# Attention with split operands: four key tiles in parts instead of two, and one rotated projection per chunk

## The reference, cut to what matters

```
x: (4, 1024, 256), 16 heads of 128
xn  = layernorm(x)
qkv = xn @ w_qkv.T;  q, k rotated (rope)
attn = softmax(q k^T / sqrt(128)) v            per sequence and head
ffn  = gelu(xn @ mxfp4(up) + up_bias) @ mxfp4(down) + down_bias
out = x + attn @ w_out.T + ffn
```

## Time and profile before

| | |
|---|---|
| median of 3 runs | 2452.34 us (2449.78 to 2453.95) |
| the profiled execution, its own time | 2450.13 us |
| its span in the profile | 2448.3 us |
| PE busy | 99% of the span |
| DVE, POOL, ACT busy | 78%, 71%, 69% |
| granted TensorE clock | 0.998 of full speed |

### The profile page before, as it was taken

One profiled execution on the slowest core, in us unless ns is written; L12 is line 12 of the kernel. 1 busy time (PEld: TensorE's weight loads), 2 busy tenths in 40 slices (PEclk: granted clock), 3 DMA queues, 4 the chain that ended last, 5 costly groups with the idle time before them and its releaser, 6 DMA issues. The chain is left out here.

```text
span 2448.3 us, 42812 instructions
## 1 busy us (share of the span) xinstructions
PE 2417.7 (99%) x13168; PEld 2124.8 (87%) x13168; DVE 1912.9 (78%) x2671; ACT 1677.9 (69%) x3039; POOL 1728.9 (71%) x1358
## 2 busy tenths in 40 slices
PE   6999999999999999999999999999999999999999
PEld 5888888888888888888888888888888888888888
DVE  6778788777877877787787778778777877877776
ACT  7767777776766777676677767667776766777533
POOL 4778877777777777777777777777777777777331
PEclk9999999999999999999999999999999999999999
DMA  4766666667666666667666666667676565666742
GB/s 140 185 170 161 171 158 178 162 162 195 182 161 149 158 152 157 157 148 195 179 161 153 157 157 148 161 149 183 165 186 157 148 162 149 157 153 161 230 153 69
DMA packets 400878, 396.72 MB, mean 162 GB/s; under 512 B 38656, under 2 KB 383104, under 8 KB 400768
## 3 DMA queue, kind: packets, MB, share of 16 engines
q1 hardware_dynamic: 400768, 395.67, 63.0%
HBM read 91.43 MB, written 35.65 MB: 52 GB/s over the span
## 5 line engine op out<-in xcount | busy, mean ns | idle before, releaser
L947 DVE TENSOR_REDUCE neg_max<-s_ps 128x1 f32<-128x1024 f32 x512 | 621.0, 1219 | 291.2 <-PE s_ps L1244 290.5
L1244 PE MATMUL s_ps<-seq_parts 128*128 128x512 f32 x3072 | 826.8, 408 | 1.4 <-DVE seq_parts L1111 0.8
L758 ACT ACTIVATE probs<-s_ps,neg_max 128x1024 f32<-128x1024 f32 x512 | 570.6, 1114 | 365.5 <-DVE neg_max L947 361.8
L1326 PE MATMUL o_ps<-keys_first,v_rows 128*128 128x256 f32 x3072 | 707.7, 380 | 1.3 <-ACT v_rows L725 1.3
L957 DVE STREAM_TRANSPOSE turned_blocks<-probs 128x1024 f32<-128x1024 f32 x512 | 630.6, 1237 | 60.6 <-ACT probs L758 38.1
L1244 PEld LDWEIGHTS s_ps<-seq_parts 128*128 128x128 f32 x3072 | 571.8, 188 | 117.2 <-ACT probs L758 1.5
L1326 PEld LDWEIGHTS o_ps<-keys_first,v_rows 128*128 128x128 f32 x3072 | 566.9, 190 | 68.6 <-ACT v_rows L725 1.7
L608 POOL TENSOR_TENSOR keys_first<-keys_first,seq_parts 128x512 fp32r<-128x512 f32 x256 | 332.4, 1298 | 320.2 <-ACT seq_parts L764 320.0
L587 POOL TENSOR_TENSOR rope_a<-rope_a,cos 128x512 f32<-128x512 f32 x252 | 325.3, 1291 | 176.9 <-ACT rope_b L740 176.7
L601 POOL TENSOR_TENSOR seq_parts<-rope_a,seq_parts 128x512 fp32r<-128x512 f32 x252 | 359.4, 1426 | 95.2 <-ACT seq_parts L750 95.1
L1244 PE MATMUL slot_ps<-seq_parts,w_parts 128*128 128x512 f32 x1506 | 387.9, 393 | 0.0
(11 more groups left out here) (118 smaller groups left out, 2597.2 us busy)
## 6 DMA issues: line engine op xcount, KB each, us to landing
keys_first<-turned_blocks SPq DMA_DIRECT2D x2048, 128.0 KB, 2.7
w_parts<-w_qkv_parts SPq DMA_DIRECT2D x72, 512.0 KB, 4.3
w_qkv_parts<-w_parts SPq DMA_DIRECT2D x24, 512.0 KB, 3.7
wo_parts<-w_out_parts SPq DMA_DIRECT2D x48, 256.0 KB, 3.1
seq_parts<-xnt_parts SPq DMA_DIRECT2D x16, 512.0 KB, 4.6
w_raw<-in_w_qkv SPq DMA_DIRECT2D x24, 256.0 KB, 4.1
seq_parts<-xnt_parts SPq DMA_DIRECT2D x6, 1024.0 KB, 8.5
y<-in_x SPq DMA_DIRECT2D x16, 256.0 KB, 3.2
```

Of the source, the lines that this page charges most:

```text
L758: nc.scalar.activation(probs[:, k2 % 4, :], s_ps[k2 % 2][:, :], ACT.Exp, bias=neg_max[:, col:col + 1], accum_out=row_sum[:, col:col + 1]). ...
L947: nc.vector.tensor_reduce(neg_max[:, k2 % 16:k2 % 16 + 1], s_ps[k2 % 2][:, :], AXX, ALU.max, negate=True).then_inc(max_ready, 1)
L1244: ins = nc.tensor.matmul(out, w, m, start=(n == 0), stop=(n == len(terms) - 1))
L1326: last = nc.tensor.matmul(out, v_rows[:, parity, kt - SPLIT, cols], keys_first[:, slot, :, kt, :].bitcast(F32), start=False, stop=(kt == B ...
```

## The change

`SPLIT` goes from 2 to 4. So `values` takes four key tiles in parts and four as f32; `probs_high` and `probs_low` each work on 1024 columns in one instruction; a second of the four v groups gets a low part on DVE; and `p_hi` and `v_lo` fill their memory, so that the feed-forward part can no longer begin before the last chunk: `G_SLOT` goes, the steps 16 and 17 keep one `up` each, and every `gelu` and `split_gelu` and all `down`s come after the steps.

`GROUPS` is written anew so that each step has one rotated group. ACT takes it, POOL makes `rotated_low` of the group before and `rotated_sum` of this one (`SUM_AT`, `LOW_AT`), and ACT makes `rotated_high` of it as the last thing of the step, now behind `probs_high`. The order of the first chunks stays (`FIRST_LATER`). Some weight and input loads move by one step.

```diff
-SPLIT = 2
+SPLIT = 4
...
-        GROUPS = {(2, 1): (0, "qk0", 0), (3, 1): (1, "qk0", 1), (4, 0): (2, "qk0", 2), (4, 1): (3, "v", 0),
-                  (5, 0): (4, "qk0", 3), (6, 0): (5, "v", 1), (6, 1): (6, "qk1", 0), (7, 0): (7, "v", 2),
-                  (7, 1): (8, "qk1", 1), (0, 0): (9, "qk1", 2), (0, 1): (10, "qk1", 3), (1, 0): (11, "v", 3)}
+        GROUPS = {(1, 1): (0, "qk0", 0), (2, 1): (1, "qk0", 1), (3, 1): (2, "qk0", 2), (4, 0): (3, "v", 0),
+                  (4, 1): (4, "qk0", 3), (5, 0): (5, "qk1", 0), (6, 0): (6, "v", 1), (6, 1): (7, "qk1", 1),
+                  (7, 0): (8, "v", 2), (7, 1): (9, "qk1", 2), (0, 0): (10, "v", 3), (0, 1): (11, "qk1", 3)}
+        SUM_AT = {2: ("qk0", 0), 3: ("qk0", 1), 4: ("qk0", 2), 5: ("qk0", 3), 6: ("qk1", 0), 7: ("qk1", 1), 0: ("qk1", 2), 1: ("qk1", 3)}
+        LOW_AT = {(k + 1) % 8: g for k, g in SUM_AT.items()}
...
POOL, a step (after probs_low):
-                if k8 == 0:
+                if first and k == 0:
                     rotated_low(p, "qk1", 0)
                     rotated_sum(p, "qk1", 1)
                     rotated_sum(p, "qk1", 2)
...
+                else:
+                    if k8 < 3 or more_pairs:
+                        rotated_low(p if k8 < 3 else p + 1, *LOW_AT[k8])
+                    if k8 < 2 or more_pairs:
+                        rotated_sum(p if k8 < 2 else p + 1, *SUM_AT[k8])
...
+                if k8 == 3 and more:
+                    w_low(p + 1, "qk1")
                 if k8 == 3 and splitting:
                     wo_low(p, 1)
-                if k8 == 4 and more:
-                    w_low(p + 1, "qk1")
...
ACT, a step (w_high of qk1 moves from step 4 to step 3; after the second exponential):
-                    if k % 8 == 3 and more_pairs:
-                        rotated_high(p + 1, "qk0", 0)
...
+                    if g and k % 8 == 5:
+                        take(0, g)
+                    probs_high(i, k)
+                    if first and k == 0:
                         rotated_high(p, "qk1", 1)
-                    if last and k == 15:
-                        act.wait_ge(bias_loaded, 32)
-                        act.wait_ge(blocks_turned, TOK * HEADS // P - 3)
-                        gelu(0, 0, True)
-                        gelu(0, 1, True)
-                        high_out(c - 1, 0)
-                    probs_high(i, k)
+                    elif k % 8 < 2 or more_pairs:
+                        rotated_high(p if k % 8 < 2 else p + 1, *SUM_AT[k % 8])
...
PE, the last steps:
-                if last and k == 15:
-                    up(0, 0, 0)
-                    up(0, 0, 1)
-                elif tail and k == 16:
-                    up(0, 0, 2)
-                    pe.wait_ge(mx_w_loaded[1], 32)
-                    pe.wait_ge(probs_ready, TOK * HEADS // P)
-                    down(0, 0, 0)
-                elif tail:
-                    down(0, 0, 1)
+                if tail:
+                    up(0, 0, k - 16)
...
-                if tail and k == 16:
-                    up(0, 0, 3)
...
+            pe.wait_ge(mx_w_loaded[1], 48)
+            pe.wait_ge(probs_ready, TOK * HEADS // P)
```

More of the change, by code:

```diff
@@ L244, in layer, with group_at @@
         V_SPLIT = tuple(n for n in range(4) if V_TILES[n] < SPLIT // 2)
-        USED = {"qk0": 5, "v": 12, "qk1": 11}
+        USED = {"qk0": 5, "v": 12, "qk1": 12}
         LN_SLOT, MX_SLOT = (5, 1), (13, 1)
         MX_PARTS = {0: (2,), 2: (3,), 3: (4,), 6: (5,), 7: (6, 7), 8: (8, 9), 10: (10,), 11: (11,), 12: (12,), 15: (0, 1)}
-        def group_at(k, slot, last):
+        def group_at(k, slot, last, first=False):
+            if first and (k, slot) in FIRST_LATER:
+                return (*FIRST_LATER[k, slot], 0)
             g = GROUPS.get((k % 8, slot))
@@ L255, in group_at @@
                 return None
-            ahead = k // 8 + (1 if k % 8 >= 2 else 0)
+            ahead = k // 8 + (1 if k % 8 >= 1 else 0)
             if last and ahead > 1:
@@ L654, in step @@
                     rotated_sum(p, "qk1", 2)
-                if k8 == 1:
+                elif first and k == 1:
                     rotated_low(p, "qk1", 1)
@@ L723, in take_group @@
                     at = 2 * V_TILES[n]
+                    tiles = bank.rearrange("p (a b) -> p a b", a=2)
                     rows = v_hi[:, parity, at:at + 2, :] if n in V_SPLIT else v_rows[:, parity, at - SPLIT:at - SPLIT + 2, :]
-                    nc.scalar.activation(rows, bank.rearrange("p (a b) -> p a b", a=2), ACT.Copy).then_inc(v_ready, 1)
+                    nc.scalar.activation(rows, tiles, ACT.Copy).then_inc(v_ready, 1)
                     return
@@ L854, in step @@
                     w_high(p + 1, "v")
+                if k % 8 == 3 and more:
+                    w_high(p + 1, "qk1")
                 if k % 8 == 3 and splitting:
                     wo_high(p, 1, first)
-                if k % 8 == 4 and more:
-                    w_high(p + 1, "qk1")
                 if k % 8 == 6 and more:
                     wo_high(p + 1, 0)
-                if tail:
-                    if k == 16:
-                        gelu(0, 2, True)
-                        gelu(0, 3, True)
-                    else:
-                        high_out(c - 2, k % 2)
-                    return
                 if not (first and k < 2):
@@ L875, in take @@
                     take_group(i * 2 + g[3], *g[:3], g[3] % 2, slot_ps[:, slot])
-                g_before = None if tail or (first and k == 0) else group_at(k - 1, 1, last)
-                if g_before and k % 8 != 1:
+                g_before = None if tail or (first and k == 0) else group_at(k - 1, 1, last, first)
+                if g_before and not (first and k == 1):
                     take(1, g_before)
@@ L933, in gelu @@
                                      bias=up_bias[:, f:f + 1]).then_inc(gelu_ready, 1)
-            steps_splitting(act, step)
-            for f in range(4, FT):
+            act.wait_ge(bias_loaded, 32)
+            act.wait_ge(blocks_turned, TOK * HEADS // P)
+            for f in range(FT):
                 gelu(0, f, True)
@@ L1195, in step @@
                         quantise(i + 1, part)
+            steps(dve, step)
             def split_gelu(g, f, first):
@@ L1224, in group @@
                 g, first = b * 2 + n, isinstance(b, int) and b == 0 and n == 0
-                for f in range(4 if first else 0, FT):
+                for f in range(FT):
                     split_gelu(g, f, first)
@@ L1268, in bank_free @@
             def bank_free(i, k, slot, first, last):
[L1271 removed]
+                for kk in (k - 1, k - 2, k - 3, k - 4):
                     if first and kk < 0:
@@ L1279, in bank_free @@
                         return
-                    g = group_at(kk % 16, slot, last and kk >= 0)
+                    g = group_at(kk % 16, slot, last and kk >= 0, first)
                     if g:
@@ L1452, in slot @@
                         return
-                    g = group_at(k, n, last)
+                    g = group_at(k, n, last, first)
                     if not g:
@@ L1495, in group @@
             def group(b, n, final):
-                for f in range(2 if b == 0 and n == 0 else 0, FT):
+                for f in range(FT):
                     if f < FT - 2:
```

68 lines of the change are left out of this document (14 added, 54 removed).

## The result

The change made the kernel slower: 2532.93 us median of four runs against 2451.65, a ratio of 1.0327 [1.0301, 1.0354]. The forecast was 2428 (2415 to 2446), so it has the wrong sign. The profiled execution took 2531.62 us, its span 2529.8.

What follows compares the result with a forecast made beforehand. PE's instruction stream was taken as the bound: -37.9 + 6 + 1.5 + 1.5 + 4.5 = -24.4 us against the profiled 2450.1 gives 2425.7; with 2.2 for the median of the runs, 2428 us, range 2415 to 2446.

Steps and rivals of the forecast that it cites:

- What bounds the kernel: Whole kernel: the length of PE's instruction stream sets the time, nearly alone; PE busy for 99% of the span.
- what PE gains: PE's values: two key tiles go from f32 to parts, 0.148 us less per chunk, 37.9 us in all.
- Parts at the f32 rate: Rival on PE's values: a part costs half an f32 instruction, 0.108 us, giving 2411 us; chance 0.03.
- no gain: Rival on PE's values: six more parts cost what four f32 instructions did, so PE saves nothing, 2464 us; chance 0.03.
- Durations off PE: ACT and POOL, per chunk: probs_high +0.49 us at 1024 columns, probs_low taken as 2.5 us.
- Is a one-group step kept?: One-group steps, sequences 1 to 3: POOL's 7.8 us fit in 8.03, high_out is on time, no loss.
- DVE held up by POOL: Rival: a third of some 80 two-input DVE instructions in one-group steps cost PE 0.5 us each, +13, 2441 us; chance 0.06.
- The hard ring: Rival, one-group steps: POOL's sum delays rotated_high, high_out and PE by 0.4 us each, giving 2478 us; chance 0.10.
- The first sequence: Steps 2 and 3 there: added weight low parts put POOL behind, PE waits 0.7 to 0.8 us a pair, +6 us.
- The start: First chunk: its low part comes 1.2 + 0.5 us later, but a wait for v stood behind; +1.5 us.
- The end: Last seven chunks without projection, +1.5 us as probs_high's extra length shows, and feed-forward work losing its cover, +4.5 us.
- the seam: Between last chunks and feed-forward part: two pieces come behind and PE waits for the first down; +4.5 us (3 to 8).

Runs made afterwards that it cites:

- places8: early8 with VectorE's quantisation comparisons spread, two instead of three in steps 7 and 8, one more each in steps 9 and 10: 2437.04 us, ratio 0.9941.
- six: Changed kernel with newton on POOL, low parts halved, quantisation in two-group steps, and six instead of eight transfers per chunk from the fifth: 2467.30 us.
- no_newton: Changed kernel without newton's four small VectorE operations, the normalisation taking the unrefined guess: 2493.51 us, ratio 1.0153.
- loop7: Changed kernel with newton on POOL, low parts halved, quantisation in two-group steps, and the loops' turn moved from step 4 to 7: 2485.62 us.
- early8: early with the loops' turn moved to step 8: 2468.42 us, ratio 1.0073.
- two mends of A: Against the changed kernel: newton moved to POOL, 2500.74 us; probs_low as two operations of 512 columns, 2496.14 us; both together, 2492.86 us.
- shadow: Changed kernel with rotated_high ahead of probs_high again and POOL's sum ahead of rotated_low: 2524.45 us, ratio 1.0303.
- six mends: On the changed kernel: newton on POOL, low parts halved, quantisation moved, probs_high per key tile, turn in step 8, comparisons spread: 2437.04 us.
- early: Changed kernel with newton on POOL, low parts halved, quantisation in two-group steps, and probs_high in two operations, one per key tile's transfers: 2481.97 us.

## Why the prediction was wrong

*What bounds the kernel, and what PE gains*: right. The stream shrank by 0.131 a step, 0.140 in a one-group step (8.033 for 8.173), against 0.148 forecast; over 256 chunks 34 instead of 37.9 us. Parts at the f32 rate and "no gain" are both out. Where nothing else is in the way (places8) the gain is there.

*Durations off PE*: right (`p_hi` +0.43 for +0.49, `probs_low` 2.41 for 2.5).

**The step that failed** is "Is a one-group step kept?", where it says that POOL starts early, "when `p_hi` comes", that `rotated_high` ends near 7.4 us, "before the step does; `high_out` behind it is then on time", and "in sequences 1 to 3 I count no loss". I took `p_hi` to come at any time that suits POOL. It can't start before its transfer lands: in the trace of before it ended a wait for the DMA 7.57 us into a step (at 1569.86), in the rows of after above 7.76 us into one. What the diff puts behind it comes later by that much: in steps 3 `high_out` starts at a median of 1.64 us, where before it was 0.39. This was to be read from the trace of before: ACT waited for that DMA 52 times, 56.6 us, with `rotated_high` in the shadow of the wait and `high_out` at 0.39. I counted the lengths of ACT's list and not the time from which it may run, and I didn't list SP's eight issues. The landing alone is worth about 22 us (six).

**The second** is the size of "DVE held up by POOL", given 0.06 and +13 us. The mechanism was right and the population wrong: I priced L1037's kin at 0.5 us each for a third of 80. The costliest are not these but newton's four operations on two columns, absent from my list because they took 0.12 to 0.17 where POOL was idle; behind a busier POOL they take 5.3 us a round, and alone are worth 39 us (no_newton). The Trainium skill, "GPSIMD Engine Reference", Key points, says that POOL shares its SBUF interfaces with VectorE and contends there with VectorE instructions that have two SBUF inputs or run in a 2-port mode; the traces agree with a contention, and show that a waiting operation ends within 0.03 us of POOL's instruction, whatever its own size. The forecast's word on `v_low`, "nothing, unless DVE is late there", is of the same kind: it asked what the new operation adds, not what the old ones meet.

**The third**, not in the prediction at all, is the turn of the loops: 20.0 us in ten gaps in ACT, much as before the change (21.9), but without slack behind it now, and 11.7 us in eight gaps in PE itself, where before there were none. Moving it alone was worth 4 us (loop7) or 14 (early8). What makes PE's gaps appear stays open.

*The hard ring*, my main rival, ended on the right side for a wrong reason: ACT's wait for POOL's sum went down, from 79.7 to 16.7 us, and POOL had 50 of 300 us free. *The first sequence*: +6 was forecast, and without the other causes 9.9 us more than before are late in all sequences together (places8), 7.8 of them in the first. *The start* was +5.2, not +1.5: PE waits 8.11 us for a projection's bank and goes on at half clock (its six matmuls take 2.93 us), where before it waited 3.13 and 1.25 us. *The end*: forecast +1.5 + 4.5, less 1.2 that the eight last chunks save, 4.8; measured 3.3 (places8 4.2). The rows of the start and of the seam, where a gelu is waited for 0.65 and a split 0.23 us:

```profile
57.39 2.93 PE L1210 MATMUL slot_ps<-seq_parts,w_parts 128*128 128x512 f32 x6 [8.11 <-ACT rope_b L734]
...
2405.87 1.15 PE L1330 MATMUL s_ps<-seq_parts,up_w 128*128 128x512 f32 x4 [0.65 <-ACT probs L905]
2407.25 1.22 PE L1343 MATMUL s_ps<-w_parts,seq_parts 128*128 128x256 f32 x8 [0.23 <-DVE seq_parts L1173]
```

One sum of the forecast was off by itself: "no gain" is 2450.1 + 13.5 + 2.2 = 2466 us, not 2464; nothing hangs on it.

How the causes share the 105 us of added late time isn't known, and may be no sum: two mends of A that gave 32 and 37 us alone gave 40 together, and newton's lock is worth 6 us in the kernel before and 39 in the changed one. Whether VectorE's small operations are free of the lock with their operands in PSUM wasn't tried, and neither was a transfer of fewer, larger pieces.

## What to carry to other kernels

For each operation that is moved, write down not only how long the engine's list is but what its first instruction waits for, transfers and their issue times above all: work ahead of such a wait is covered by it, the same work behind it makes what follows late by its length (though moving it back, in shadow, gained 8 us only, since the other engines' work moves too). When POOL (GpSimd) gets busier or its instructions longer, look for the tiny VectorE operations that stand in a chain, keep POOL's instructions short, and put the chain on POOL itself or where slack stands behind it. Look for gaps that nothing in the profile explains where a loop turns, on every engine. And take causes away one on top of the other before judging a change: here six mends, of which the two tried alone still left 2496 and 2501 us, turned 3.3% slower into 0.6% faster.

## What the runs showed of the hardware that I had not expected

- A VectorE operation on 128x2 elements in SBUF takes 0.12 to 0.17 us beside an idle POOL and ends with POOL's running instruction otherwise: 1.18 to 1.64 us in the rows above. L1019, on 128x8, took a mean of 1.78. The evictions from PSUM (`low_out`, 0.38 to 0.42) didn't change beside a busy POOL, nor did the transpose of 1024 columns (L931, 1.20 to 1.25 in all of its 512).
- Two POOL operations of 512 columns (1.30 each) in place of one of 1024 (2.41) made this kernel 37 us faster, though they take longer.
- A wait of PE of 2.59 us was followed by 3.4 us at a granted clock of 0.53, close to the lower level of 1.2 GHz, so that it cost more than its own length.
- The turn of a loop showed as about 2 us without an instruction on ACT (20.0 us in ten gaps), and in some kernels as a gap on PE in each of 14 rounds (13.7 us in loop7, 19.7 in early, a mean of 1.0 and 1.4), in others not at all (before, early8).
